# Normalizing between attention and feed-forward: scaling on VectorE instead of ScalarE and GpSimd, with a new order of steps

## The reference

```python
x = hidden_states                                    # (1, 2048, 256)
x = x + layernorm(attention(layernorm(x)))
x = x + layernorm(ffn(layernorm(x)))
```

## Time and profile before

| | |
|---|---|
| time, median of 3 runs | 1406.82 us (1406.25 to 1407.59) |
| the profiled execution's own time | 1406.82 us |
| its span in the profile | 1405.0 us |
| TensorE busy | 1355.8 us (96%) |
| VectorE busy | 1017.9 us (72%) |
| ScalarE busy | 892.8 us (64%) |
| GpSimd busy | 875.1 us (62%) |
| granted TensorE clock | 1.00 of full speed in all stretches below |

### The profile page before, as it was taken

The page is one execution under the profiler, slowest core; times in us unless marked ns, Lnnn a source line. Parts: engine busy times, 40 slices in busy tenths (PEclk is TensorE's granted clock), DMA queues, the critical chain, the costliest instruction groups (busy, mean ns, idle before and its releaser), DMA issues.

```text
span 1405.0 us, 26355 instructions
## 1 busy us (share of the span) xinstructions
PE 1355.8 (96%) x8280; PEld 1198.9 (85%) x8280; DVE 1017.9 (72%) x2564; ACT 892.8 (64%) x2503; POOL 875.1 (62%) x1370
## 2 busy tenths in 40 slices
PE   5799999999999999999999999999999999999998
PEld 4679999988989999888889999888889888887887
DVE  5677778777677777767777788767678888855544
ACT  5467766766567667666666666665667777655442
POOL 2457666664757665555666756546767778758454
PEclk9999999999999999999999999999999999999999
DMA  3000000000000000000000000000100000000001
GB/s 131 2 31 1 1 1 1 1 16 1 1 31 1 1 1 1 1 16 2 31 1 1 1 1 1 20 1 1 46 1 1 22 26 1 17 30 1 27 15 35
DMA packets 9751, 18.49 MB, mean 13 GB/s; under 512 B 912, under 2 KB 7312, under 8 KB 9104
## 3 DMA queue, kind: packets, MB, share of 16 engines
q1 hardware_dynamic: 8272, 15.23, 3.2%
q10 hardware_dynamic: 1344, 1.57, 0.3%
HBM read 14.71 MB, written 2.10 MB: 12 GB/s over the span
## 4 chain that ended last, share of the span: by engine, by line
PE 75%; DVE 9%; POOL 7%; ACT 6%; issue 3%; DMA 0%; ACTq 0%; POOLq 0%; DVEq 0%
PE turn_bank L691 8%; PE score_bank L669 7%; PE score_bank L671 7%; PE score_bank L670 7%; PE score_bank L786 5%; PE sum_bank L691 4%; PE turn_bank L693 4%; PE turn_bank L678 3%; PE proj_bank L691 3%; PE turn_bank L737 3%; PE turn_bank L751 2%; ACT e L815 2%; PE sum_bank L693 2%; PE proj_bank L678 2%; POOL e L1257 2%
## 5 line engine op out<-in xcount | busy, mean ns | idle before, releaser
L815 ACT ACTIVATE e<-score_bank,negmx 128x512 f32<-128x512 f32 (+2 forms) x640 | 394.5, 626 | 82.2 <-DVE negmx L1029 81.5
L1257 POOL TENSOR_TENSOR e<-e,e 128x512 f32<-128x512 f32 (+3 forms) x256 | 295.7, 1155 | 21.4
L1025 DVE TENSOR_REDUCE mx<-score_bank 128x1 f32<-128x512 f32 (+1 forms) x384 | 244.8, 639 | 23.9 <-PE score_bank L671 22.9
L669 PE MATMUL score_bank<-k_hi,q_hi 128*128 128x512 f32 (+2 forms) x640 | 253.3, 396 | 7.8 <-ACT e L815 5.8
L1240 POOL TENSOR_TENSOR inv_s<-s,neg_one 128x1 f32<-128x1 f32 x128 | 71.1, 555 | 299.7 <-DVE s L1224 299.2
L671 PE MATMUL score_bank<-k_hi,q_lo 128*128 128x512 f32 (+2 forms) x640 | 231.7, 362 | 0.0
L670 PE MATMUL score_bank<-k_lo,q_hi 128*128 128x512 f32 (+2 forms) x640 | 231.1, 361 | 0.0
L691 PE MATMUL turn_bank<-v_hl,pT_hi 128*128 128x512 f32 x588 | 217.3, 403 | 5.6 <-DVE pT_lo L1035 5.5
L1254 POOL TENSOR_SCALAR e<-e,ratio 128x512 f32<-128x512 f32 (+3 forms) x256 | 178.1, 696 | 12.0
L1020 DVE CUSTOM_DVE_ANT_0 score_bank<-score_bank,mask 128x384 f32<-128x384 f32 (+3 forms) x256 | 143.4, 560 | 49.2 <-PE score_bank L671 47.8
L693 PE MATMUL turn_bank<-v_hl,pT_lo 128*128 128x256 f32 x588 | 165.0, 281 | 0.0
(11 more groups left out here) (347 smaller groups left out, 3551.3 us busy)
## 6 DMA issues: line engine op xcount, KB each, us to landing
w_raw<-in_w_qkv_dram SPq DMA_DIRECT2D x3, 1024.0 KB, 4.8
w_raw<-in_w_o_dram SPq DMA_DIRECT2D x4, 512.0 KB, 3.2
w_raw<-in_w_ug_dram SPq DMA_DIRECT2D x4, 512.0 KB, 3.9
bv<-in_hidden_dram SPq DMA_DIRECT2D x8, 256.0 KB, 3.0
out_dram<-e SPq DMA_DIRECT2D x16, 128.0 KB, 1.7
e<-in_w_d_dram SPq DMA_DIRECT2D x1, 1024.0 KB, 4.9
x_in<-in_hidden_dram SPq DMA_DIRECT2D x2, 256.0 KB, 3.8
x_in<-in_hidden_dram ACTq DMA_DIRECT2D x2, 256.0 KB, 4.2
```

Of the source, the lines that this page charges most:

```text
L669: pe.matmul(bank[:, 0:w], qh, kh, start=True, stop=False)
L815: act.activation(e, S[k % NS][:, 0:w], ACT.Exp, bias=negmx[:, d % 2, m, s:s + 1], accum_out=ssum[:, d % 4, s, m, c:c + 1]).then_inc(s_act, 1)
L1025: dve.tensor_reduce(mx[:, d % 2, m, s, c:c + 1], S[k % NS][:, 0:w], X, ALU.max)\
L1257: pool.tensor_tensor(a, a, b, ALU.add).then_inc(p_pool, 1)
```

## The change

Part 1 and part 3 go to VectorE, and the step NA is gone. Part 1 is now two operations of VectorE per tile: acc = acc * n_rs + input, and then acc = acc - n_rs * mean; the product n_rs * mean (`n_mr`) comes from GpSimd. Part 3 is one operation per tile, (acc - mean) * n_rs. GpSimd keeps three small operations after part 0 and two after part 2. With one step pair less per chunk, chunks 0 and 1 take the N tokens of halves 13 to 17 and 21 to 25, the b of half 19 moves to 18, the last halves hold 9 U instead of 12 in another order, and `with_gated` places the steps of chunks 2 and 3 and the folds anew.

```diff
-              16: 'TSSTSSTPNTSfoQTPPNPTO', 17: 'TSTSSNOSTPSfoQNTPPTP', 18: 'TSSTSSTPNTSfoQTPPNPTO',
-              19: 'TSTSSbOSTPSoQTPbPTP', 20: 'TSSTSSTPTSfoQTPPPTO', 21: 'TSTSSNOSTPSfoNQTPPTP',
...
-              25: 'TSTSSNOSTPSoQNTPPTP', 26: 'TSSTSSTPNTSfoQTPPNPTO', 27: 'TSTSSOSTPSfoQTPPTP',
...
-LAST_HALVES = ('UToTUPTUToOUP', 'UTUTOTUPUPTPO', 'UToTUTTUOoPUo')
+              16: 'TSSTSSTPNTSfoQTPPNPTO', 17: 'TSTSSNOSTPSfoQNTPPTP', 18: 'TSSTSSTPbTSfoQTPPbPTO',
...
+              26: 'TSSTSSTPTSfoQTPPPTO', 27: 'TSTSSOSTPSfoQTPPTP', 28: 'TSSTSSfTPbTSfoQTPPbPTO',
...
+LAST_HALVES = ('ToTPTToOPUU', 'UTUTOTPUPTPO', 'TUoTUTTOUoPUo')
...
-    norms = [x for c in range(2) for x in norm_steps(c, (0, 1, "add", 2, 3)) + turn_steps(c)]
+    norms = [x for c in range(2) for x in norm_steps(c, range(4)) + turn_steps(c)]
...
-        3: norm_steps(2, (0,)) + [("DB", 0), ("DB", 1)], 4: [("DB", 2), ("DB", 3)],
-        5: norm_steps(2, (1,)) + [("DB", 4), ("DB", 5)], 6: norm_steps(2, ("add",)) + [("DB", 6), ("DB", 7)],
-        7: [("DB", 8), ("DB", 9)], 8: norm_steps(2, (2,)) + [("DB", 10), ("DB", 11)], 9: [("DB", 12), ("DB", 13)],
-        10: [("DB", 14), ("DB", 15)], 11: norm_steps(2, (3,)) + [("FH", 8), ("FH", 9)],
+        2: norm_steps(2, (0,)), 4: norm_steps(2, (1,)) + [("DB", 0), ("DB", 1)], 5: [("DB", 2), ("DB", 3)],
+        6: norm_steps(2, (2,)) + [("DB", 4), ("DB", 5)], 7: [("DB", 6), ("DB", 7)], 8: norm_steps(2, (3,)),
+        9: [("DB", i) for i in range(8, 12)], 10: [("DB", i) for i in range(12, 16)], 11: [("FH", 8), ("FH", 9)],
         12: [("F", 8), ("F", 9), ("FH", 10), ("FH", 11)], 13: [("F", 10), ("F", 11)], 14: turn_steps(2),
-        16: norm_steps(3, (0,)), 17: norm_steps(3, (1,)), 18: norm_steps(3, ("add",)), 20: norm_steps(3, (2,)),
-        22: norm_steps(3, (3,))}
+        16: norm_steps(3, (0,)), 18: norm_steps(3, (1,)), 20: norm_steps(3, (2,)), 22: norm_steps(3, (3,))}
...
-                    elif kind == "N" and what[1] % 2 == 1:
-                        c, part, half = what
-                        act.wait_ge(z_rstd if part == 3 else y_rstd, c + 1)
...
+                        elif part == 1:
+                            dve.wait_ge(y_rstd, c + 1)
+                            dve.wait_ge(xr_landed, 32 * c + 32)
+                            for x, t in pair:
+                                dve.scalar_tensor_tensor(out=acc[:, t, :], in0=acc[:, t, :], scalar=n_rs[:, x:x + 1],
+                                                         in1=z[:, x, :], op0=ALU.mult, op1=ALU.add)\
+                                   .then_inc(n_step, 1)
+                            dve.wait_ge(n_step, base + 2)
+                            for x, t in pair:
+                                dve.tensor_scalar(acc[:, t, :], acc[:, t, :], n_mr[:, x:x + 1], None, ALU.subtract)\
+                                   .then_inc(n_step, 1)
                         else:
...
+                            dve.wait_ge(z_rstd, c + 1)
+                            for x, t in pair:
+                                dve.tensor_scalar(z[:, x, :], acc[:, t, :], n_mv[:, x, 0:1], n_rs[:, x:x + 1],
+                                                  ALU.subtract, ALU.mult).then_inc(z_ready, 1)
...
-                        pool.tensor_scalar(n_neg[:, :], n_mv[:, :, 0], -1.0, 0.0, ALU.mult, ALU.add)\
-                            .then_inc(n_pool, 1)
...
+                            pool.tensor_tensor(n_mr[:, :], n_rs[:, :], n_mv[:, :, 0], ALU.mult).then_inc(y_rstd, 1)
...
-                    elif kind == "NA":
-                        c, half = what
-                        pool.wait_ge(n_scaled, QB * c + 2 * half + 2)
-                        pool.wait_ge(xr_landed, 32 * c + 32)
-                        for x in (2 * half, 2 * half + 1):
-                            t = chunk_tiles(c)[x]
-                            pool.tensor_tensor(acc[:, t, :], acc[:, t, :], z[:, x, :], ALU.add).then_inc(n_added, 1)
```

More of the change, by code:

```diff
@@ L166, in norm_steps @@
     def norm_steps(c, parts):
-        return [("NA", (c, half)) if part == "add" else ("N", (c, part, half)) for part in parts for half in range(2)]
+        return [("N", (c, part, half)) for part in parts for half in range(2)]
     def turn_steps(c):
@@ L375, in build @@
             n_rs = sa("n_rs", [P, QB])
-            n_neg = sa("n_neg", [P, QB])
-            n_shift = sa("n_shift", [P, QB])
+            n_mr = sa("n_mr", [P, QB])
             def raw_w(f):
@@ L477, in build @@
                 att, "had_step", "had_ready", "scales_ready", "folded_ready", "wt_hi_ready", "wt_lo_ready", "xr_landed",
-                "n_step", "n_scaled", "n_added", "n_pool", "y_rstd", "z_rstd", "z_ready", "wsd_landed", "wd_landed", "wd_pool", "wd_dve",
+                "n_step", "n_pool", "y_rstd", "z_rstd", "z_ready", "wsd_landed", "wd_landed", "wd_pool", "wd_dve",
                 "g_full", "u_full", "g_act", "h_ready", "h_hi_ready", "h_lo_ready", "d_full", "d_half_ready",
@@ L1168, in _ @@
                                           xT_hi[:, ct, zc].bitcast(F32), ALU.subtract).then_inc(t_lo, 1)
-                    elif kind == "N" and what[1] % 2 == 0:
+                    elif kind == "N":
                         c, part, half = what
-                        base = 16 * c + 4 * part + 4 * half
+                        base = 24 * c + 8 * part + 4 * half
                         pair = [(x, chunk_tiles(c)[x]) for x in (2 * half, 2 * half + 1)]
@@ L1174, in _ @@
                             dve.wait_ge(r_free, max(r_use["OP", last_visit[t]] for _, t in pair) + 1)
-                            if c > 0:
-                                dve.wait_ge(z_rstd, c)
-                        else:
[L1178 to L1183, removed]
+                        if part in (0, 2):
+                            dve.wait_ge(n_step, base)
+                            for x, t in pair:
+                                dve.bn_stats(n_stats[:, x, :], acc[:, t, :]).then_inc(n_step, 1)
+                            dve.wait_ge(n_step, base + 2)
+                            for x, t in pair:
+                                dve.bn_aggr(n_mv[:, x, :], n_stats[:, x, :]).then_inc(n_step, 1)
+                        elif part == 1:
[5 more added lines that the diff above has]
+                                   .then_inc(n_step, 1)
+                            dve.wait_ge(n_step, base + 2)
+                            for x, t in pair:
+                                dve.tensor_scalar(acc[:, t, :], acc[:, t, :], n_mr[:, x:x + 1], None, ALU.subtract)\
+                                   .then_inc(n_step, 1)
+                        else:
+                            dve.wait_ge(z_rstd, c + 1)
+                            for x, t in pair:
+                                dve.tensor_scalar(z[:, x, :], acc[:, t, :], n_mv[:, x, 0:1], n_rs[:, x:x + 1],
+                                                  ALU.subtract, ALU.mult).then_inc(z_ready, 1)
                     elif kind == "DB" and what >= 8:
@@ L1327, in _ @@
                         c, part, _ = what
[L1328 to L1331, removed]
+                        pool.wait_ge(n_step, 24 * c + 8 * part + 8)
                         pool.tensor_scalar(n_var[:, :], n_mv[:, :, 1], 1.0, EPS, ALU.mult, ALU.add)\
                             .then_inc(n_pool, 1)
-                        pool.tensor_scalar(n_neg[:, :], n_mv[:, :, 0], -1.0, 0.0, ALU.mult, ALU.add)\
-                            .then_inc(n_pool, 1)
-                        pool.wait_ge(n_pool, step + 2)
-                        pool.tensor_tensor(n_rs[:, :], n_var[:, :], half_neg[:, :], ALU.pow).then_inc(n_pool, 1)
-                        pool.wait_ge(n_pool, step + 3)
-                        pool.tensor_tensor(n_shift[:, :], n_neg[:, :], n_rs[:, :], ALU.mult)\
-                            .then_inc(z_rstd if part else y_rstd, 1)
-                    elif kind == "NA":
-                        c, half = what
-                        pool.wait_ge(n_scaled, QB * c + 2 * half + 2)
-                        pool.wait_ge(xr_landed, 32 * c + 32)
-                        for x in (2 * half, 2 * half + 1):
-                            t = chunk_tiles(c)[x]
-                            pool.tensor_tensor(acc[:, t, :], acc[:, t, :], z[:, x, :], ALU.add).then_inc(n_added, 1)
+                        pool.wait_ge(n_pool, 3 * c + (2 if part else 0) + 1)
+                        if part == 0:
+                            pool.tensor_tensor(n_rs[:, :], n_var[:, :], half_neg[:, :], ALU.pow).then_inc(n_pool, 1)
+                            pool.wait_ge(n_pool, 3 * c + 2)
+                            pool.tensor_tensor(n_mr[:, :], n_rs[:, :], n_mv[:, :, 0], ALU.mult).then_inc(y_rstd, 1)
+                        else:
+                            pool.tensor_tensor(n_rs[:, :], n_var[:, :], half_neg[:, :], ALU.pow).then_inc(z_rstd, 1)
                     elif kind == "DB" and what < 8:
```

12 lines of the change are left out of this document (5 added, 7 removed).

## The result

The changed kernel takes 1418.43 us (median of 4 runs, 1417.42 to 1420.91), the kernel before on the same chip 1406.53 (4 runs, 1405.90 to 1407.59). The ratio is 1.0086, with an interval from 1.0073 to 1.0098: slower by some 12 us. The profiled execution took 1416.04 us, its span is 1414.2. The forecast of 1409.7 was too low, and the time lies above its range.

What follows compares the result with a forecast made beforehand. TensorE was taken as the bound (busy 1355.8 of 1405.0 us), so only its idle time could move. Attention +2.3, last halves 0, folds +0.6 and chunk 3 0 gave +2.9 on 1406.82: 1409.7 us, range 1404.0 to 1415.0.

Steps and rivals of the forecast that it cites:

- prediction's own signs of being wrong: No new TensorE waits for VectorE before 1200, new operations over 1 us in the mean, or wait before F8 gone.
- Length: New VectorE operations alone: 0.467 us per multiply-add, 0.354 per subtraction or scaling; 4.1 us of VectorE per chunk with overlap.
- 0.23 us per new operation: Interference price of each new VectorE operation beside a busy GpSimd; bounds 0 and 0.9 us.
- The attention: Chunks 0 and 1: TensorE loses 2.2 and 1.2 us to late VectorE and wins 1.1, together +2.3 us.
- "1.2 us" of tolerance: Attention: VectorE may be 1.2 us late before TensorE stops; taken off 3.4 (chunk 0) and 2.4 us (chunk 1).
- Won: Attention: TensorE waits for xT_lo, oT_lo and the mix, together 2.3 us, go; half counted, 1.1 us.
- The last halves: End of attention: +1.7 us wait for o_sum, -0.8 for the pT_lo wait, smaller waits give back some; put at 0.
- The folds: Down-weight folds start after U4, not U3; F8 at 1297.1 against 1296.55, +0.6 us, bounds -1.8 and +3.0.
- rival 2: GpSimd mattered: its relief brings F8 1.8 us sooner, with attention waits -3.1 us, 1403.7 us; chance 0.16.
- Chunk 3 and the tail: After 1300: 4.1 us more of VectorE hidden behind some 20 us of gate products, 0; at most 4.1 us uncovered.
- Rival 3: The lock in full: every new operation waits out a GpSimd operation (0.65 us each), folds 3 us later, 1418 us; chance 0.15.
- Rival 1: Lateness absorbed in VectorE's gaps: half of 3.4 us lost, 2.3 won in full, 0.6 at folds, 1406.8 us; chance 0.27.

Runs made afterwards that it cites:

- e2: Changed kernel's new order of steps, with the division of work of the kernel before (ScalarE scales, GpSimd adds): 1411.63 us, ratio 1.0023.
- e3: Changed kernel with each of the 48 new VectorE operations replaced by a bn_stats into small tiles, x1 and z not formed: 1411.06 us, ratio 1.0022.
- e5: Kernel before with only the new strings for halves 16 to 28 (chunks 0 and 1 one step pair less); old division, last halves and folds: 1403.11 us.
- e6: e5 with the changed kernel's last halves (9 gate and up products instead of 12); old table for chunks 2 and 3 and folds: 1407.51 us.
- e1: Changed kernel's division of work (scaling and adding on VectorE) in the order of steps of the kernel before: 1418.0 us, ratio 1.0073.
- e4: Changed kernel with part 3 alone back on ScalarE, part 1 staying on VectorE, new order: 1417.26 us, ratio 1.0070.
- e8: Changed kernel measured and profiled again with no edit, for scatter: 1418.38 us, ratio 1.0079 against the kernel before.

## Why the prediction was wrong, step by step

None of the prediction's own signs of being wrong appeared: TensorE has new waits for VectorE before 1200, the new operations stay under 1 us in the mean, and the wait before F8 is there. The direction was right, and the sum too small.

**The price of an operation.** Length: right, but for 0.05 us in part 3. Interference "0.23 us per new operation": right in the attention (0.24) and too low beside the folds, where it was 0.57 for each of 12 operations. There GpSimd runs operations of 1.3 us back to back. VectorE (first three rows, start and duration) and GpSimd in the profile after:

```profile
1274.59 0.74 DVE L1203 SCALAR_TENSOR_TENSOR v_sum<-score_bank,col,w_raw 128x512 f32<-128x512 f32 x1
1275.25 2.53 DVE L1174 SCALAR_TENSOR_TENSOR acc<-acc,n_rs,bv 128x256 f32<-128x256 f32 x2
1277.81 2.57 DVE L1179 TENSOR_SCALAR acc<-acc,n_mr 128x256 f32<-128x256 f32 x2
...
1274.77 2.72 POOL L1347 TENSOR_TENSOR e<-e,out_b_row 128x512 f32<-128x512 f32 x2
1277.46 1.47 POOL L1359 TENSOR_TENSOR k_lo<-v_sum,k_hi 128x512 fp32r<-128x512 f32 x1
1278.89 2.64 POOL L1347 TENSOR_TENSOR e<-e,out_b_row 128x512 f32<-128x512 f32 x2
```

Four VectorE operations of 0.4 us need 5.1 us while four of GpSimd pass: between two of VectorE one of GpSimd gets in each time. The gated product of 0.74 us, which reads a PSUM bank, keeps its time. These lines agree with the rule of the Trainium skill (SBUF — State Buffer, Who interferes with whom) by which the later one fully blocks, for the single-input tensor_scalar too. The forecast took its lower bound from "later operations of a burst may hold what the first has won": they do not.

**The attention: +2.3 forecast, +4.2 measured.** Both terms were off. *Lost*: 2.2 and 1.2 us were forecast for chunks 0 and 1. Against e2, which has the same order, the change loses 4.3 and 3.5 us: 1.3 each by length (e3 less e2), 3.0 and 2.2 by blocking (after less e3). The new operations of chunk 0 were stretched by 3.5 us and those of chunk 1 by 2.4, so an amount near all of the blocking reached TensorE. The step that failed is the "1.2 us" of tolerance: I took it off the whole sum. What the runs show is that of a length spread over the halves most is absorbed (1.3 of the 4.5 us of a chunk's bn_stats arrive), and of stretched operations in the middle of a burst little is. The tolerance is not all of it: without it the sums would be 3.4 and 2.4 us, still 0.9 and 1.1 short. And the half behind the first stretch was to have "no time to catch up" at 8.8 us of work; it had 10.40 us in it, and ran 1.5 us longer. *Won*: I counted half of 2.3 us; e5 shows 3.3, more than the three waits themselves.

**The last halves: 0 forecast, +1.2 measured** (e2 the same, so it is the order; e6 shows only 0.3). The wait for o_sum, put at 1.7 us, is there with 1.5 at its longest and 2.4 in two; what was to balance it was less.

**The folds: +0.6 forecast, +4.8 measured.** This step failed most, and not by blocking: the order alone has +5.1 (e2). e6 assigns 3.4 to the last halves: with three products fewer ahead of the end of the attention, three more follow it among the folds, and their splits stand behind folds and additions in GpSimd's queue. The first wait for v_sum in e6 (1.5 us) and the first two in e2 (0.8 and 1.1) end with a gated product ahead of which VectorE was idle for 4.20, 4.95 and 2.53 us, waiting for GpSimd's split. GpSimd was the bound there, as in the earlier trace rows, and the prediction counted its time up to the last fold, but not what its splits free for VectorE and so for TensorE. That the three products are the reason for the full queue is argued, not shown. The lower clock at F8 is the other part of the 3.4 us. Why the clock falls in e6 and not in e5, at the same wait, stays open; what differs ahead of it is the two waits of 1.5 and 0.5 us for v_sum in e6.

The other 1.7 us (e2 less e6) come with the new table, in which VectorE makes four folds in a row (steps 9 and 10) instead of two. VectorE after the change:

```profile
1294.80 4.19 DVE L1193 TENSOR_TENSOR e<-e 128x512 f32<-128x512 f32 x4
1298.91 0.75 DVE L1203 SCALAR_TENSOR_TENSOR v_sum<-score_bank,col,w_raw 128x512 f32<-128x512 f32 x1
1299.57 2.97 DVE L1193 TENSOR_TENSOR e<-e 128x512 f32<-128x512 f32 x3
```

The product that frees TensorE's bank stands behind 4.19 us of folds: this is the longer wait for v_sum, 1.7 of the 2.8 us; the other 1.1 ends with the gated product behind a single fold (1.77 us at 1292.44). The kernel before has 0.2 us of such waits. I priced only the date of F8, by adding the work ahead of it ("nine operations, 6.2 us"), and neither the bank that the gated product gives back nor the clock behind the wait, 1.4 us, for which the prediction has no term. The first fold of GpSimd came at 1274.77, not at the 1270.4 I had put it at, but 3.8 us of this are what TensorE had lost by then (5.4, less the 1.6 by which this execution began half 14 earlier than the one before). And the eight VectorE folds took 1.14 us in the mean, not 0.69, beside GpSimd's splits. e3, with the same order but nothing of the old division, loses 2.7 here: the move does relieve this place by 2.4 us, as rival 2 had it (1.8), and blocking takes 2.1 back.

**Chunk 3 and the tail: 0 forecast, +0.6 measured.** 0.5 to 0.6 us appear after the folds in every kernel with the new last halves. They are no wait: each of the down steps 5 to 15 takes 0.05 us longer, a few ns in each of its products, and I have no cause for them. (The 0.5 of e1 is another: it comes at once, between down steps 3 and 4.)

**The rivals.** Rival 3 gave the time, 1418, with a chance of 0.15. Its mechanism holds beside the folds, where operations wait out a whole GpSimd operation, and not in the attention, at 0.24 us each and not 0.65. That the time agrees is luck: its sum came out right since in the attention blocking reaches TensorE almost in full and since the order costs 3.6 us that it did not have. Rival 1 (absorbed) holds only for the length. Rival 2's relief is real and small. None of the rivals had the order itself as a cause, which e2 shows to be a third of the loss.

**The best version.** e5 takes the part of the change that pays. Whether the new division with the old last halves and an unbunched table would be worth anything was not run as such; its attention alone is 7.6 us behind e5's.

Three things stay open: the 0.6 us above; why the runs of the changed kernel scatter by 3 to 4 us while its two profiles agree (the longest runs have the lowest mean granted clock, 0.992 at 1421.75 us against 0.996 at 1416.04, so more stretches at half the clock are likely, but none of the long ones was profiled); and why most medians (e1, e4 to e8) stand 0.7 to 1.7 us better against before than the table, in which each kernel is one execution.

## What to carry to other kernels

Before short elementwise work is moved to VectorE, look at what GpSimd does at that time: beside back-to-back GpSimd operations of 1.3 us, VectorE operations of 0.35 to 0.47 us on SBUF took about 1.3 us each, and where VectorE was already some 80% full TensorE lost nearly as much as the stretching came to (5.2 of 5.8 us). Price an in-order queue by what stands right behind the bunch (the operation that frees a bank, or the split that frees a buffer for it), not by the date at which the bunch ends. Read the granted clock behind the waits as well: 3.4 us at half of it cost 1.4 us here. And when a change moves work and reorders steps, run the two halves apart: here the order's first part alone gained 0.3%, its second part lost that and more, and the move lost the most.

## What the runs showed of the hardware

- A tensor_scalar with one SBUF input and two scalars per partition (128x256, float32) took 0.40 us alone and up to 1.46 beside GpSimd. The Trainium skill (VectorE: DVE Perf Modes, Mode 2×_2P — use both read ports for one tensor) lets it run in a mode that uses both read ports; that it was held up agrees with that.
- Neither engine holds the other back for a whole burst: VectorE and GpSimd took turns, operation by operation (2.53 us for two operations of 0.47).
- bn_stats of the same tensor was not held at all: 48 of them at 0.41 to 0.42 us in the mean in the same places (e3).
- TensorE's granted clock fell to half for 3.4 us around the end of the wait at F8: after 1.54 us of work in 4.2 us (the change) and after 2.22 in 4.2 with two more waits ahead of them (e6), but not after 1.83 in 4.2 in the kernel before. A product of 512 columns then took 0.43 us from start to start instead of 0.23.
- TensorE's losses behind a fixed step repeat within 0.3 us between executions (after, e8), although the executions differ by some 3 us ahead of it. Such a table tells apart what medians of four runs cannot, as long as the granted clock of both executions is compared too.
